# A two-layer transformer on one Trainium2 core: small matmuls of the local attention cut into halves, a feed-forward product moved, and the final pass drawn into the drain of the loop

## The reference, cut to what matters

```python
for i in range(DEPTH):                                   # DEPTH = 6
    x = attn_layer(shift_tokens(x), Wqkv[i], q_scale[i], k_scale[i], Wo[i]) + x
    x = ffn_layer(shift_tokens(x), ln_g[i], ln_b[i], W1[i], b1[i], W2[i], b2[i]) + x
...
# attn_layer: q, k of unit length, scaled and rotated; then for each window of 32
sim = jnp.einsum('bhwie,bhwje->bhwij', bq, bk2) * QK_SCALE      # scores, 32 x 64
attn = jax.nn.softmax(jnp.where(mask, -big, sim), -1)
out = jnp.einsum('bhwij,bhwje->bhwie', attn, bv2)               # values
...
# ffn_layer: layer norm, then
a * gelu(gate) @ W2 + b2
...
x = x + gb * _L1_ffn_ref(h, ...)                                # the final sum
```

## Time and profile before

| | |
|---|---|
| median of 3 runs | 2651.61 us (2647.77 to 2654.76) |
| the profiled execution, its own time | 2656.48 us |
| its span, first to last instruction | 2654.7 us |
| mean granted TensorE clock | 0.913 of full speed |
| TensorE busy | 2149.8 us (81%), 34508 matmuls and as many weight loads |
| VectorE, ScalarE, GpSimd busy | 1845.5, 1481.8, 1544.7 us |
| chain that ended last, by engine | PE 41%, issue 32%, DVE 17%, ACT 7% |

### The profile page before, as it was taken

How to read it: one execution, slowest core, us unless ns; L and a number is a source line. 1 busy time by engine, 2 the same in 40 slices (tenths; PEclk the granted TensorE clock), 3 DMA queues, 4 the chain that set the end, 5 groups by cost and what they waited for, 6 DMA issues and landing times.

```text
span 2654.7 us, 87198 instructions
## 1 busy us (share of the span) xinstructions
PE 2149.8 (81%) x34508; PEld 1550.1 (58%) x34508; DVE 1845.5 (70%) x3811; ACT 1481.8 (56%) x2864; POOL 1544.7 (58%) x797
## 2 busy tenths in 40 slices
PE   4888865789757898888878888888878988888885
PEld 2554443564435666666656666566666666666663
DVE  4674555664546777777778877778868877777873
ACT  1672334562334565666566665666656666666662
POOL 0110001110018888888878888788978888778870
PEclk9998877888767899999999999999999999999997
DMA  4000001000001222322232222222232222322220
GB/s 89 2 1 1 1 1 45 1 2 0 1 1 47 64 60 52 83 68 64 50 87 57 72 55 57 75 77 60 54 87 57 72 58 54 79 73 55 59 64 17
DMA packets 94723, 126.36 MB, mean 48 GB/s; under 512 B 27484, under 2 KB 42466, under 8 KB 94306
## 3 DMA queue, kind: packets, MB, share of 16 engines
q1 hardware_dynamic: 94306, 120.54, 18.1%
HBM read 21.91 MB, written 1.05 MB: 9 GB/s over the span
## 4 chain that ended last, share of the span: by engine, by line
PE 41%; issue 32%; DVE 17%; ACT 7%; POOL 2%; DVEq 0%; SPq 0%; ACTq 0%; DMA 0%; POOLq 0%
PE pj L526 11%; PE oo L526 9%; PE sc L526 9%; PE tr L529 8%; ACT arena L1369 6%; DVE arena L1206 3%; DVE arena L1212 3%; PE tr L526 2%; DVE arena L1204 2%; DVE xn L955 1%; PE oo L529 1%; DVE arena L1237 1%; DVE slab L1247 1%; DVE arena L1097 1%; ACT hT L1369 1%
## 5 line engine op out<-in xcount | busy, mean ns | idle before, releaser
L1369 ACT ACTIVATE arena<-tr 128x512 f32<-128x512 f32 (+2 forms) x880 | 464.0, 570 | 292.5 <-PE tr L529 265.7
L1681 POOL TENSOR_TENSOR arena<-arena 128x1024 f32<-128x1024 f32 x192 | 456.4, 2377 | 230.9 <-DVE arena L1206 219.0
L1683 POOL TENSOR_TENSOR arena<-arena,half_neg 128x16 f32<-128x16 f32 x192 | 564.0, 2937 | 0.0
L529 PE MATMUL tr<-ident,arena 128*128 128x128 f32 x3024 | 467.3, 292 | 104.5 <-ACT arena L1369 31.0
L1369 ACT ACTIVATE arena<-pj 128x512 f32<-128x512 f32 x576 | 335.5, 595 | 311.7 <-PE pj L526 284.2
L529 PEld LDWEIGHTS tr<-ident,arena 128*128 128x128 f32 x3024 | 368.2, 148 | 204.2 <-issue 74.2
L1204 DVE TENSOR_TENSOR arena<-pj,rtab 128x512 f32<-128x512 f32 x384 | 263.3, 686 | 315.5 <-ACT arena L1369 301.4
L1689 POOL TENSOR_TENSOR arena<-arena 128x1024 f32<-128x1024 f32 x192 | 365.5, 1904 | 24.6
L1369 ACT ACTIVATE arena<-arena 128x1024 f32<-128x1024 f32 (+4 forms) x424 | 281.9, 668 | 163.4 <-DVE arena L1087 70.3
L1649 POOL TENSOR_TENSOR rstd<-rstd,half_neg 128x4 f32<-128x4 f32 x40 | 40.5, 1012 | 546.7 <-DVE rstd L950 546.5
L1206 DVE TENSOR_TENSOR arena<-pj,rtab 128x512 f32<-128x512 f32 x384 | 261.5, 681 | 0.0
(11 more groups left out here) (205 smaller groups left out, 3983.9 us busy)
## 6 DMA issues: line engine op xcount, KB each, us to landing
slab<-arena SPq DMA_DIRECT2D x576, 128.0 KB
slab<-arena SPq DMA_DIRECT2D x336, 64.0 KB
wqkv<-in_L_ffn_Wqkv SPq DMA_DIRECT2D x18, 512.0 KB, 3.7
wo<-in_L_ffn_Wo SPq DMA_DIRECT2D x6, 512.0 KB, 4.2
w<-in_L_ffn_W SPq DMA_DIRECT2D x6, 341.0 KB
arena<-in_L_attn_x SPq DMA_DIRECT2D x4, 256.0 KB, 2.9
arena<-in_L_ffn_W SPq DMA_DIRECT2D x1, 1024.0 KB
out_x<-xn SPq DMA_DIRECT2D x4, 256.0 KB, 2.3
```

The costliest lines, as they stand in the source:

```text
L529: return nc.tensor.transpose(o, i, ident[0:i.shape[0], 0:i.shape[0]])
L1369: return nc.scalar.activation(o, i, f, **k)
L1681: p_.tensor_tensor(r_, r_, rb[:, k, :], ALU.add).then_inc(sum_ok, 1)
L1683: p_.tensor_tensor(rr[:, k, :], rr[:, k, :], half_neg[:, 0:HL], ALU.pow).then_inc(pow_ok, 1)
```

## The change

1. `window_scores` and `values` take a half i: four head pairs each (64 MATMUL and 64 LDWEIGHTS in the trace). The second half alone updates `sc_mm` or `o_mm`. The first half of the values waits for the first half of the turned probabilities alone, the first half of the scores for three of the four q and k parts.
2. What stands between. Values: first half, `turn_k`, then in t = 0 and 1 chunk 3 and the second half; in t = 2 and 3 the second half, chunk 3 and chunk 4. Scores: first half; then chunk 4 (t = 0), chunk 4 and `turn_out` (t = 1), `turn_out` (t = 2, 3); then the second half. `norm_back` of t = 3 stands behind.
3. The down product of slot t = 1 stands between the second half of the values and the first half of the scores, in `tr[:, 1]`. Its addition on VectorE stands behind `clamp(g, 1)`, ahead of `soft1`. ScalarE's mask waits for it no more; the second half of `turn_out` does (`y_ff`).
4. The final pass: `final_sum` (one VectorE instruction a batch), `final` (four turns, into `pj`), `final_copy` and a store each have buffers of their own (`fin`, `fout`). Batches 0, 1 and 2 stand between the drain slots, batch 3 behind them.

```diff
-            def window_scores(g, t):
-                pe.wait_ge(qk_cp, g * 4 + 4)
-                pe.wait_ge(masked, g + 1)
+            def window_scores(g, t, i):
+                pe.wait_ge(qk_cp, g * 4 + 3 + i)
+                if i == 0:
+                    pe.wait_ge(masked, g + 1)
                 apart(pe)
-                for pr in range(PAIRS):
+                for pr in range(4 * i, 4 * i + 4):
...
-            def values(n, g, t):
-                pe.wait_ge(pt_cp, g * 2 + 2)
+            def values(n, g, t, i):
+                pe.wait_ge(pt_cp, g * 2 + 1 + i)
...
+                        if t == 1 and j == 1 and m2 is not None:
+                            pe.wait_ge(y_ff, m2 + 2)
                         turn_out(g - 2, j)
...
                 if d_:
-                    values_()
+                    values_(0)
                 if c_:
                     turn_k()
+                if t in (2, 3) and d_:
+                    values_(1)
                 if new:
                     project(g, t, 3)
+                if t in (2, 3):
+                    value_part(4)
+                elif d_:
+                    values_(1)
                 if t == 0 and m2 is not None:
                     if c_:
                         pe.wait_ge(qk_cp, g * 4)
                     ff_up(m2, 1)
+                if t == 1 and m2 is not None:
+                    pe.wait_ge(qk_cp, g * 4 if c_ else NTILE * 4)
+                    ff_down(m2)
                 if c_:
-                    window_scores(g - 1, (t - 1) % T)
-                if new:
-                    project(g, t, 4)
+                    window_scores(g - 1, (t - 1) % T, 0)
+                if t in (0, 1):
+                    value_part(4)
+                if t != 0 and d_:
+                    out_()
+                if c_:
+                    window_scores(g - 1, (t - 1) % T, 1)
+                if t == 0 and m2 is not None:
+                    pe.wait_ge(on_ok, g - 1 if d_ else NTILE)
+                    ff_up(m2, 2)
+                if t == 0 and d_:
+                    out_()
...
+            def final(b):
+                pe.wait_ge(x_fin, b + 1)
+                if b >= 2:
+                    pe.wait_ge(f_cp, b - 1)
+                for t in range(T):
+                    last = tp(pj[:, b % 2, t * P:(t + 1) * P], fin[:, b, t * P:(t + 1) * P])
+                last.then_inc(f_tr, 1)
+            def after(i):
+                for b in ((0, 1), (2,), ())[min(i, 2)]:
+                    final(b)
...
+            def final_sum(b):
+                if b == 0:
+                    ve.wait_ge(sum_ok, NTILE * 2)
+                ve.wait_ge(y_ff, (DEPTH - 1) * B + b + 2)
+                v.scalar_tensor_tensor(out=fin[:, b, :], in0=YT[:, b * S:(b + 1) * S],
+                                       scalar=modT[:, b, 6 + GB:7 + GB], in1=XT[:, b * S:(b + 1) * S],
+                                       op0=ALU.mult, op1=ALU.add).then_inc(x_fin, 1)
...
-                    if t == 1 and m2 is not None:
-                        ac.wait_ge(y_ff, m2 + 2)
...
```

More of the change, by code:

```diff
@@ L378, in run_slots @@
                 slot(Slot(DEPTH, 0, t))
+                if after is not None:
+                    after(t)
             for t in range(2):
@@ L506, in _ @@
             out_v = out.rearrange("b (t p) k -> b p t k", p=P)
-            with sp.Fori(0, B) as b:
+            for b in range(B):
                 sp.wait_ge(f_cp, b + 1)
-                sp.dma_start(out_v[bass.ds(b, 1)].rearrange("a p t k -> (a p) t k"), xn[:, :, :]
-                             ).then_inc(st_out, 16)
+                sp.dma_start(out_v[b], fout[:, b, :].rearrange("p (t k) -> p t k", k=P)).then_inc(st_out, 16)
             sp.wait_ge(st_out, 16 * B)
@@ L854, in wo_half, with ff_down, value_part @@
                     last.then_inc(wo_mm, 1)
+                def ff_down(m):
+                    for k, (o, w) in enumerate(CH):
+                        pe.wait_ge(ff_ev, m * FFC + 3)
+                        last = mm(tr[:, 1], w2[0:w, k, :], fa[0:w, k, :], start=(k == 0), stop=(k == FFC - 1))
+                    last.then_inc(w2_mm, 1)
+                def value_part(c):
+                    if new:
+                        if b == 0 and t == 0 and c == 4:
+                            pe.wait_ge(wl_ok[2], l + 1)
+                        project(g, t, c)
                 if new:
@@ L870, in slot @@
                     ff_up(m2, 0)
-                if t in (1, 2) and (m1, m2)[t % 2] is not None:
+                if t == 2 and m1 is not None:
                     pe.wait_ge(t_sub, g - 1 if c_ else NTILE)
-                if t == 1 and m2 is not None:
[L874 to L878, removed]
                     wo_half(m1, 1)
@@ L904, in slot @@
                     norm_back(LNB, LNB_BANKS[1], m1)
[L905 to L909, removed]
                 if t == 2 and m1 is not None:
@@ L920, in slot @@
                     wo_half(n, 0)
+            def final(b):
[8 more added lines that the diff above has]
+                    final(b)
             for u in range(2):
                 mm(sc[:, u], ident[:, :], YT[:, 0:S])
[L924 to L932, removed]
+            run_slots(pe, slot, after)
+            final(B - 1)
         @block.vector
@@ L1302, in slot @@
                     add_attention(0)
-                if t == 1 and m2 is not None:
-                    y = YT[:, s_.y2:s_.y2 + S]
-                    ve.wait_ge(w2_mm, m2 + 1)
-                    apart(ve)
-                    v.scalar_tensor_tensor(out=y, in0=sc[:, 0], scalar=lcur[:, 2:3], in1=y,
-                                           op0=ALU.add, op1=ALU.add).then_inc(y_ff, 1)
                 if t == 2 and m1 is not None:
@@ L1330, in slot @@
                     ff_gate(m2, 1)
+                if t == 1 and m2 is not None:
+                    y = YT[:, s_.y2:s_.y2 + S]
+                    ve.wait_ge(w2_mm, m2 + 1)
+                    apart(ve)
+                    v.scalar_tensor_tensor(out=y, in0=tr[:, 1], scalar=lcur[:, 2:3], in1=y,
+                                           op0=ALU.add, op1=ALU.add).then_inc(y_ff, 1)
                 if c_:
```

52 lines of the change are left out of this document (28 added, 24 removed).

## The result

The changed kernel took **2626.97 us** (median of 4 runs, 2618.49 to 2632.59), the kernel before 2653.19 us beside it (2647.77 to 2657.89): ratio **0.990**, 95% interval 0.986 to 0.994. Timed again beside later runs it took 2627.56 us, where the kernel before took 2666.05: ratio 0.984 (0.982 to 0.987). So the gain was 26 us in the first comparison and 38 in the second, not 98. The kernel before has medians of 2653 to 2672 us in the five comparisons, the changed kernel 2627.0 and 2627.6 in its two. Medians are of fast runs; the only slow one, of `d_all` with 2688.73 us at a granted clock of 0.805, is left out.

What follows compares the result with a forecast made beforehand. TensorE was taken as nearest its limit, with 23.0 us a layer of pauses read as late instruction fetch. From 2656.5 us: -84 - 34 + 25 + 19 - 14 - 10 = -98, less 4.9 for the median: 2554 us, range 2518 to 2612.

Steps and rivals of the forecast that it cites:

- "issue" in values and scores: Sign of being right: TensorE idle time without shown reason there falls from 58 us in three layers to some 20.
- the wait of 2 us in t = 1: Sign of being right: TensorE idles about 2 us ahead of the turned probabilities of t = 1, ended by ScalarE.
- the short end: Sign of being right: some 5.5 us from the last addition to the end.
- The down product leaves its gap: Slot t = 1: moving the product leaves TensorE idle, +1.1 us a slot, 23 slots: +25 us (0 to +50).
- Halves: Values and scores: work between halves covers instruction fetch, removing 14.3 us of pauses a layer: -84 us (nothing to -136).
- What follows a pause: TensorE slots: a pause costs 1.4 times its length, with turns at the lower clock behind it: another -34 us.
- Two more runs: Two more runs of small matmuls a slot, 0.1 us each for semaphores and halts: +19 us (0 to +45).
- The values waited: Values: the first half needs one of ScalarE's two copies, saving half of 4.6 us a layer: -14 us.
- Later scores: Scores' second half ends up to 1.6 us later in t = 2 and 3, hidden by VectorE's own lateness: no cost.
- The first rival: VectorE and ScalarE's chain from the scores' end becomes the bound; 50 us given back, 2604 us; chance 0.17.
- The final pass: Kernel's end: one round left instead of four, -12.3, and +2.6 for batch 2's turns; together -10 us (-14 to -5).

Runs made afterwards that it cites:

- d_all: Changed kernel with the down product, the norm's turns of t = 3 and chunk 4 of t = 2 and 3 moved back: 2573.84 us, ratio 0.964 to before.
- e_near: As d_all, with the turns of the output also back behind the scores' second half; only halves and new final pass left: 2564.13 us, ratio 0.963 to before.
- m_down_only: Kernel before the change, with the move of the down product alone: 2710.02 us, ratio 1.015.
- a_down: Changed kernel with the down product of t = 1 back ahead of the turned probabilities, with its addition and waits: 2598.26 us, ratio 0.973 to the kernel before.
- j_shift: Kernel before the change, with 128 more instructions on TensorE ahead of the slots and nothing else: 2666.28 us against 2660.34, ratio 1.002.
- h: Kernel before the change, with only the values split in halves around the k turns (t = 0, 1: also chunk 3): 2592.24 us, ratio 0.972.
- f_final: Kernel before the change, with the new final pass alone: 2649.33 us, ratio 0.994.

## Why the prediction was wrong

The direction and the mechanism of the halves were right, the size was not, and the time lies above the range. Against 98 us forecast, the changed kernel gained 38 beside the parts. Of some 60 us that are missing, 19 are the down product (44 instead of 25), 22 the norm's turns (instead of nothing), and 21 lie in all other terms together: 102 us in `e_near` instead of 123. The direction was clear of noise, and of what was to show the forecast right most came: "issue" in values and scores fell from 58 to 10 us in three layers, the longest pause in small matmuls is 1.5 us, the wait of 2 us in t = 1 and the short end are there. A layer of 281 to 286 us (300 measured) and a mean granted clock above 0.93 (0.922) did not come.

1. **"The down product leaves its gap", +25 us: the step that failed.** The mechanism was the one named, the price was 44 us by itself. The net of 1.1 us a slot was too small. The terms shown give 2.6 - 0.45 - 0.47 - 0.24 = 1.4; the other 0.3 was for ScalarE's mask, which stands just ahead of the copies that the scores wait for with those 0.47, so it may be the same saving counted twice (not shown). Measured are 1.7 us a slot at a granted clock of 1.00: 16.6 us in `m_down_only` against 14.9 before, and 17.3 in the changed kernel against 15.6 in `a_down`. Besides, the wait of 2.0 us is followed by the lower clock in half of these slots. In `m_down_only` six slots without a pause take 17.5 to 17.8 us at a clock of 0.90, six take 16.6 to 16.7 at 1.00; in the changed kernel it is 8 and 8, with 0.8 us between them. I gave pauses a factor for that, and the new wait none. As an estimate, 23 x (1.7 + 0.4) is 48 us. The bound of +50 held.
2. **The norm's turns of t = 3 were priced at nothing, and the prediction does not name them**, though the list of the change does: 22 us alone, 27 us undone on the changed kernel. This is the second step that failed. The diff moves them behind the second half of the scores; ScalarE's order then holds the output copies behind them.
3. **"Halves", -84.** The mechanism is shown by `j_shift` and the packets: at the end of a block of 256 instructions TensorE stops for up to 3.8 us. The Trainium skill (Runtime: NRT & Kernel Launch, Instruction fetch mechanics) calls the crossing "mostly hidden"; in these small matmuls the trace does not agree. The changed kernel's pauses even fell by 18.2 us a layer instead of 14.3. But it owes part of that to its moved steps, which stand between dense runs: with them undone, in `e_near`, "issue" is 48.6 us in four layers against 25.4, so 12.4 a layer less than before. Between these two kernels the moves (with chunk 4 and the turns of the output, which stand elsewhere too) bought 23 us in four layers, and cost 54 us of waits and 19 of busy time there.
4. **"What follows a pause", -34.** Nothing of it came: the granted clock of the four layers is 0.97 before and after. The new waits took the place of the pauses: slots t = 1 with a granted clock of 0.91 are 8 of 16, where before it was 1 of 16. With the waits undone the clock rises, to 0.99 in `e_near`:

```profile
1067.09:2216.65 1149.56, 1034.95 (x20531) 763.10 (x20529) 928.26 (x1552) 753.49 (x1252) 989.28 (x469) 0.99 0.27 69
```

5. **"Two more runs", +19.** Busy time rose by 7.6 us over four layers in `e_near`, with 128 runs more: 0.06 us each where I took 0.1. The clock was higher there, which works the other way; no run separates the two.
6. **"The values waited", -14.** Held for what it counted: in h the wait for ScalarE ahead of the values fell by 8.8 us in four layers, where the term has 9.5. The wait ahead of the turned probabilities fell by another 7.6, which the term does not have.
7. **"Later scores", nothing.** Not decided: the intervals of d and e overlap, but e is 10 us lower, and its slots t = 1 and t = 3 without a pause are shorter (14.9 and 18.8 us against 15.6 and 19.3). The first rival was right that ScalarE is waited for in t = 1 and t = 3 and near in price (50 us), but in the main not by its chain from the scores. It was the steps taken out of the gap and put ahead of ScalarE's input.
8. **"The final pass", -10.** From the last addition's end (2625.84) to the end of the span 5.0 us are left, 5.5 forecast, 17.8 before. The part that failed is the +2.6 for the turns of batch 2 ahead of the last projection. `f_final` gave 17 us (12 to 21 by its interval), and its trace shows where more than the 12.8 at the end came from: in the 15 us that end with that projection the granted clock is 1.00 where it was 0.77 before, and the projection takes 3.62 us instead of 5.38. That the turns which now stand in gaps of the drain keep the clock up is likely, not tested. The row of `f_final`:

```profile
2615.04 3.62 PE L529 MATMUL sc<-arena,wo 128*128 128x256 f32 x16
```

In the changed kernel it takes 4.84. The last rows of the changed kernel:

```profile
2625.09 0.75 DVE L1363 SCALAR_TENSOR_TENSOR YT<-tr,lcur,YT 128x512 f32<-128x512 f32 x1 [3.11 <-PE tr L529]
2625.87 0.75 DVE L1385 SCALAR_TENSOR_TENSOR arena<-YT,modT,XT 128x512 f32<-128x512 f32 x1
...
2627.38 0.69 DVE L1392 COPY arena<-pj 128x512 f32<-128x512 f32 x1 [0.75 <-PE pj L532]
```

With moves undone the forecast would have been 98 + 25 = 123 us; e gave 102, or 98 by its ratio. What the moves cost is 66 us instead of 25. The first layer of slots lost less to the moves (276.4 us, 274.4 with the down product back, 272.4 with the norm's turns back), where each of the four behind it gained 6 by either. The pipeline is filling there: it has two down products instead of four and three of the norm's turns instead of four, for which 3.1 and 4.4 us would be due.

## What to carry to other kernels

Price every step that a change moves, also one that the diff moves in passing: ask for each what its old place filled, and which engine takes its result first in order and holds what else behind it. A new wait costs more than its length where the lower clock follows it, as in half of the slots here, so where waits replace pauses nothing is gained, clock included. Split a change into its parts and time them alone: here one part, the values in halves, gave twice what the whole gave, and two moves took back two thirds of what the rest gained.

## What the runs showed that was not expected

- The pauses are tied to the program's position alone: 128 instructions more ahead of the loop moved every one of them to other matmuls, and the medians are 0.2% apart (`j_shift`). All 150 in three kernels end 1.1 to 1.6 us after a packet of the instruction queue has landed.
- A wait of TensorE for ScalarE of 2.0 us is followed by the lower clock in some places and not in others (8 of 16 slots t = 1 of the changed kernel), and moving one product of 2.6 us out of such a gap, without adding work, lowered the mean granted clock of four layers from 0.97 to 0.94 and lengthened them by 56 us in the profiled executions (`m_down_only`; by medians the whole kernel took 44 us more).
- The kernel with long pauses differs by 0.7% from comparison to comparison (medians of 2653 to 2672 us; 2660 to 2672 on the four chips of the experiments), the changed one by 0.6 us in 2627 in two. Why wasn't looked into.
